# Three attention layers of 16 heads x 8: maxima by halves of 8 heads, one clamp per head, weights on three semaphores

## What is computed

```python
# L0 cross attention (512 keys, 96 wide); x is (8, 256, 128), 16 heads of 8
q = (layernorm(x) @ Wq + bq).reshape(B, Nq, H, D).transpose(0, 2, 1, 3)
k = (ctx @ Wk + bk).reshape(B, Nkv, H, D).transpose(0, 2, 1, 3)
v = (ctx @ Wv + bv).reshape(B, Nkv, H, D).transpose(0, 2, 1, 3)
attn = jnp.einsum('bhqd,bhkd->bhqk', q, k) * D ** -0.5
attn = jnp.clip(attn, -10000.0, 10000.0)
attn = jax.nn.softmax(attn, axis=-1)
x = x + jnp.einsum('bhqk,bhkd->bqhd', attn, v).reshape(B, Nq, Cq) @ Wo + bo
```

## Time and profile before

| | us |
|---|---|
| median of 3 runs | 2920.61 |
| lowest, highest | 2910.09, 2923.78 |
| the profiled execution | 2914.34 |
| its span, first to last instruction | 2912.6 |

### The profile page before, as it was taken

How to read it: one execution, slowest core, us unless ns; L and a number is a source line. 1 busy time by engine, 2 the same in 40 slices (tenths; PEclk the granted TensorE clock), 3 DMA queues, 4 the chain that set the end, 5 groups by cost and what they waited for, 6 DMA issues and landing times. The chain is left out here.

```text
span 2912.6 us, 40706 instructions
## 1 busy us (share of the span) xinstructions
PE 2224.6 (76%) x13779; PEld 1382.4 (47%) x13779; DVE 1690.1 (58%) x3810; ACT 1174.3 (40%) x2898; POOL 522.7 (18%) x703
## 2 busy tenths in 40 slices
PE   4668888789996897534799994936888886898982
PEld 2424343367774454423566663625555654344441
DVE  5568999633434562877456556562665554754524
ACT  3114444445552564211344441410555553354550
POOL 1122220000002410121111101011333322212100
PEclk9759999899997898866899997965999998698995
DMA  0043323110002310000000001011000001332200
GB/s 27 12 116 86 115 77 92 50 40 1 1 1 62 76 46 28 8 0 0 31 1 1 1 1 28 1 27 34 1 1 1 1 1 38 85 75 63 53 11 17
DMA packets 109272, 95.63 MB, mean 33 GB/s; under 512 B 61414, under 2 KB 96526, under 8 KB 105742
## 3 DMA queue, kind: packets, MB, share of 16 engines
q1 hardware_dynamic: 75790, 91.99, 12.2%
q10 hardware_dynamic: 33280, 1.05, 0.5%
HBM read 77.21 MB, written 14.81 MB: 32 GB/s over the span
## 5 line engine op out<-in xcount | busy, mean ns | idle before, releaser
L920 DVE TENSOR_REDUCE L_xattn_mx<-L_xattn_psS 128x1 f32<-128x512 f32 x512 | 326.9, 684 | 152.9 <-PE L_xattn_psS L1045 148.7
L1160 ACT ACTIVATE L_xattn_PT<-L_xattn_psT 128x512 f32<-128x512 f32 x512 | 284.7, 598 | 170.8 <-PE L_xattn_psT L1057 163.6
L1071 PE MATMUL L_xattn_psO<-L_xattn_PT,L_xattn_V 128*32 128x256 f32 x2048 | 264.1, 404 | 40.8 <-DVE L_xattn_PT L931 40.8
L588 ACT ACTIVATE L_attn_pr<-L_attn_psS,L_attn_negm 128x256 f32<-128x256 f32 (+1 forms) x512 | 222.4, 447 | 175.4 <-PE L_attn_psS L511 92.0
L1045 PE MATMUL L_xattn_psS<-L_xattn_KR,L_xattn_QR 72*128 72x512 bf16 x512 | 224.0, 441 | 56.3 <-DVE L_xattn_mx L920 30.0
L1057 PE MATMUL L_xattn_psT<-L_xattn_QR,L_xattn_KR 75*128 75x256 bf16 x1024 | 198.7, 283 | 3.0 <-ACT L_xattn_PT L1160 2.0
L1875 DVE TENSOR_TENSOR L_ffn_wt<-L_ffn_act,L_ffn_cw 128x512 f32<-128x512 f32 x128 | 88.5, 692 | 183.8 <-ACT L_ffn_act L1992 172.4
L1071 PEld LDWEIGHTS L_xattn_psO<-L_xattn_PT,L_xattn_V 128*32 128x32 f32 x2048 | 118.4, 115 | 154.6 <-issue 61.2
L931 DVE SCALAR_TENSOR_TENSOR L_xattn_PT<-L_xattn_PT,L_xattn_floor_w 128x512 f32<-128x512 f32 x256 | 178.4, 741 | 16.1 <-DMA L_xattn_floor_w<-L_xattn_staged_floor 11.6
L392 DVE TENSOR_REDUCE L_attn_mx<-L_attn_psS 128x2 f32<-128x512 f32 x256 | 164.4, 684 | 40.0 <-PE L_attn_psS L501 40.0
L415 DVE TENSOR_TENSOR L_attn_aoT<-L_attn_raw,L_attn_psOR 128x256 f32<-128x256 f32 x128 | 54.0, 422 | 222.7 <-ACT L_attn_raw L601 222.7
(11 more groups left out here) (537 smaller groups left out, 4342.8 us busy)
## 6 DMA issues: line engine op xcount, KB each, us to landing
L_xattn_KR<-L_xattn_k_parts SPq DMA_DIRECT2D x96, 192.0 KB
L_xattn_floor_w<-L_xattn_staged_floor SPq DMA_DIRECT2D x8, 2048.0 KB, 8.2
L_xattn_QR<-L_xattn_q_parts SPq DMA_DIRECT2D x32, 288.0 KB
L_xattn_k_parts<-L_xattn_ks SPq DMA_DIRECT2D x48, 128.0 KB, 2.6
L_xattn_ctxT<-in_ctx SPq DMA_DIRECT2D x24, 192.0 KB, 2.4
L_attn_QR<-L_attn_q_parts SPq DMA_DIRECT2D x16, 288.0 KB
L_attn_KR<-L_attn_k_parts SPq DMA_DIRECT2D x48, 96.0 KB
L_xattn_q_parts<-L_xattn_qs SPq DMA_DIRECT2D x48, 64.0 KB, 2.5
```

Of the source, the lines that this page charges most:

```text
L588: ins = nc.scalar.activation(pr[n % 3][:, r, t, 0:width], psS[(2 * n + r) % 3][:, t, 0:width], ACT.Exp, bias=negm[:, n % 4, t, r:r + 1], s ...
L920: nc.vector.reduce_max(mx[:, b % 2, u, hd:hd + 1], psS[n % 2][:], AX.X).then_inc(s_used, 1)
L1071: ins = nc.tensor.matmul(psO[r:r + HW, g % 2], V[b % NV][:, kt, n % H], PT[(n * NU + kt // 2) % NPT][:, kt % 2], start=(kt == 0), stop=(kt ...
L1160: nc.scalar.activation(PT[i % NPT][:], psT[i % NPS][:], ACT.Exp).then_inc(exp_ready, 1)
```

## The change

It is made of these parts:

- LEAD goes from H to HH = 8 heads plus the same margin: 14 instead of 22 (18 instead of 26 in L1); PREP from 42 to 38 (60 to 52).
- Job M and the rows are done twice a batch, each for 8 heads. The half i is at step 16b + 8i - 5 (16b + 8i - 9 in L1). negm, mp, floor and floor_w are half as high; the rows have a semaphore for each half.
- In from_ctx layers the order is K, T, Q instead of T, Q, K, with K at 16b - 38, T one step behind it and Q two; stage and spread take k first. Stage is at 16b - 33. Within a step M is sorted behind the other jobs.
- A PT tile holds a head's four key tiles, five of them instead of ten half as large, and one clamp covers 1024 columns.
- The weights have three semaphores: for q and k, for v, and for the output. PE waits for each ahead of its first use.
- POOL sets V[0] between norm(0) and norm(1), and the other V tiles behind DVE's splits of the first batch. It adds bo at Q instead of K.

```diff
...
-    NPS, NPT = 3, 10 if NU == 2 else 8
+    NPS, NPT = 3, 5 if NU == 2 else 8
...
-    LEAD, PREP, STAGE, DVE_SPLITS = (H + 6, 42, 3, 2) if from_ctx else (H + 10, 60, 6, 3)
+    LEAD, PREP, STAGE, DVE_SPLITS = (HH + 6, 38, 3, 2) if from_ctx else (HH + 10, 52, 6, 3)
...
         at = prep_step(b)
-        for i, kind in enumerate("TQK"):
+        for i, kind in enumerate("KTQ" if from_ctx else "TQK"):
             jobs[at + i * (b > 0)].append((kind, b, 0))
         jobs[max(H * b - LATE_V, FIRST) if from_ctx else at + 3 * (b > 0)].append(("V", b, 0))
-        jobs[H * b - LEAD + H + 1].append(("M", b, 0))
+        for i in range(2):
+            jobs[H * b + HH * i - LEAD + HH + 1].append(("M", b, i))
         for i in range(NO):
...
-        stage_at = at + 2 + STAGE if b else FIRST
+        stage_at = min(at + 2 + STAGE, prep_step(b + 1) + 1) if b else FIRST
         moves[stage_at].append(("stage", b, 0))
         moves[max(stage_at, H * (b - NB + 1) + 1)].append(("spread", b, 0))
-        moves[H * b - LEAD + H + 1].append(("rows", b, 0))
+        for i in range(2):
+            moves[H * b + HH * i - LEAD + HH + 1].append(("rows", b, i))
         if head_major:
...
-    jobs[FIRST].sort(key=lambda job: job[1])
+    for n in jobs:
+        jobs[n].sort(key=lambda job: (job[0] == "M", job[1] if n == FIRST else 0))
...
-        negm, mp = sb("negm", [H, S]), sb("mp", [H, PARTS, S], BF16)
-        PT = [sb(f"PT{i}", [P, 2, S]) for i in range(NPT)]
+        negm, mp = sb("negm", [HH, S]), sb("mp", [HH, PARTS, S], BF16)
+        PT = [sb(f"PT{i}", [P, NKT, S]) for i in range(NPT)]
...
-        floor, floor_w = (sb("floor", [H, S]), [sb(f"floor_w{i}", [P, H, S]) for i in range(2)]) if clamp else (None, None)
-        minus_clamp = sb("minus_clamp", [H, 1]) if clamp else None
-        f_dram = nc.dram_tensor(f"{pre}_staged_floor", (H, S), F32, kind="Internal").ap() if clamp else None
+        floor, floor_w = (sb("floor", [HH, S]), [sb(f"floor_w{i}", [P, HH, S]) for i in range(2)]) if clamp else (None, None)
+        minus_clamp = sb("minus_clamp", [HH, 1]) if clamp else None
+        f_dram = nc.dram_tensor(f"{pre}_staged_floor", (HH, S), F32, kind="Internal").ap() if clamp else None
...
-        NLOAD = 8 if bq is not None else 5
+        WQK, WV = (4, 2) if bq is not None else (2, 1)
...
+            loads = [(wk_s[:], m.dram[wk], qk_loaded), (wq_s[:], m.dram[wq], qk_loaded)]
...
+            loads += [(wv_s[:], m.dram[wv], v_loaded), (wo_s[:], m.dram[wo], o_loaded), (bo_s[:], rows(m.dram[bo]).to_broadcast((P, D)), o_loaded)]
+            for dst, src, done in loads:
+                sp.dma_start(dst, src).then_inc(done, 16)
...
+                if from_ctx:
+                    stage_k()
+                    stage_q()
+                else:
+                    stage_q()
+                    stage_k()
...
+                for hf in range(2):
+                    heads, done = slice(hf * HH, (hf + 1) * HH), regrouped[b % 2][hf]
+                    if from_ctx:
+                        spread_k(heads, done)
+                        spread_q(heads, done)
+                    else:
+                        spread_q(heads, done)
+                        spread_k(heads, done)
...
+            def max_rows(b, hf):
+
+                n = 2 * b + hf
                 wait(sp, st_ready, NU * H * (b - NB + 1))
-                sp.wait_ge(m_split, b + 1)
+                sp.wait_ge(m_split, n + 1)
                 for i in range(PARTS):
-                    sp.dma_start(QR[b % NB][PAIR + i:PAIR + i + 1], mp[:, i]).then_inc(m_rows, 16)
...
                     sp.dma_start(f_dram, floor[:]).then_inc(floor_staged, 16)
-                    sp.wait_ge(floor_staged, 16 * (b + 1))
...
+                    wait(sp, clamped, HH * (n - 1))
+                    sp.dma_start(floor_w[n % 2][:].rearrange("p h s -> p (h s)"),
+                                 rows(f_dram.rearrange("h s -> (h s)")).to_broadcast((P, HH * S))).then_inc(floor_spread, 16)
...
-            def split_max(b):
-
-                pool.wait_ge(negm_ready, b + 1)
+            def split_max(n):
+
+                pool.wait_ge(negm_ready, n + 1)
                 if clamp:
                     link(nc.gpsimd.tensor_scalar(negm[:], negm[:], clamp, None, ALU.min))
                     nc.gpsimd.sem_inc(clamp_set, 1)
+                    if n >= 1:
+                        pool.wait_ge(m_rows[(n - 1) % 2], 16 * PARTS * ((n - 1) // 2 + 1))
                     link(nc.gpsimd.tensor_copy(mp[:, 0], negm[:]))
-                    pool.wait_ge(floor_ready, b + 1)
...
             norm(0)
+            nc.gpsimd.memset(V[0][:], 1.0).then_inc(v_set, 1)
             norm(1)
-            for i in range(NV):
+            pool.wait_ge(k_split, SPLITS)
+            pool.wait_ge(q_split, SPLITS)
+            for i in range(1, NV):
                 nc.gpsimd.memset(V[i][:], 1.0).then_inc(v_set, 1)
...
                     if kind == "T" and b >= 2:
                         norm(b)
                     if kind == "Q" and b >= DVE_SPLITS:
                         split_q(nc.gpsimd, link, b)
                     if kind == "K" and b >= DVE_SPLITS:
                         split_k(nc.gpsimd, link, b)
-                    if kind == "K":
+                    if kind == "Q":
                         add_bo(b)
                     if kind == "M":
-                        split_max(b)
+                        split_max(2 * b + i)
...
-                b, hd = n // NU // H, n // NU % H
-                dve.wait_ge(exp_ready, n + 1)
-                if n % (NU * H) == 0:
-                    dve.wait_ge(floor_spread, 16 * (b + 1))
+                half = n // HH
+                dve.wait_ge(exp_ready, NU * (n + 1))
+                if n % HH == 0:
+                    dve.wait_ge(floor_spread, 16 * (half + 1))
                 at = PT[n % NPT][:]
-                nc.vector.scalar_tensor_tensor(at, at, 1.0, floor_w[b % 2][:, hd, None, :].to_broadcast((P, 2, S)), ALU.min, ALU.max).then_inc(clamped, 1)
-
-            def bound_max(b):
-
...
+            def bound_max(b, i):
+
+                await_job(dve, ("M", b, i))
+                wait(dve, m_split, 2 * b + i)
+                nc.vector.tensor_scalar(negm[:], psM[0:HH, 0:S], -1.0, -clamp, ALU.mult, ALU.max).then_inc(psM_read, 1)
+                await_read(dve, ("M", b, i))
...
-            pe.wait_ge(loaded, 16 * NLOAD)
-
...
-                    pe.wait_ge(s_used, NSU * (b + 1))
+                    pe.wait_ge(s_used, NSU * b + NSU // 2 * (i + 1))
...
+                if b == 0 and kind in "QK":
+                    pe.wait_ge(qk_loaded, 16 * WQK)
+                if b == 0 and kind == "V":
+                    pe.wait_ge(v_loaded, 16 * WV)
+                if b == 0 and kind == "O":
+                    pe.wait_ge(o_loaded, 16 * 2)
...
-                        ins = nc.tensor.transpose(psM[0:H, t * P:(t + 1) * P], mx[:, b % 2, t], m.ident[:])
+                        ins = nc.tensor.transpose(psM[0:HH, t * P:(t + 1) * P], mx[:, b % 2, t, i * HH:(i + 1) * HH], m.ident[:])
...
-                if hd == 0 and u == 0:
-                    pe.wait_ge(m_rows, 16 * PARTS * (b + 1))
+                if hd % HH == 0 and u == 0:
+                    pe.wait_ge(m_rows[hd // HH], 16 * PARTS * (b + 1))
...
+                        if n >= NPT:
+                            act.wait_ge(pv_done, (n - NPT) // 2 + 1)
+                        nc.scalar.activation(PT[n % NPT][:, 2 * u:2 * u + 2], psT[i % NPS][:], ACT.Exp).then_inc(exp_ready, 1)
...
```

More of the change, by code:

```diff
@@ L762, in spread, with spread_q @@
             def spread(b):
                 wait(sp, st_ready, NU * H * (b - NB + 1))
[L765 to L767 removed]
+                def spread_q(heads, done):
+                    sp.wait_ge(q_staged, 16 * PARTS * (b + 1))
                     src = q_dram[b % 2].rearrange("i d h c -> (i d) h c")[:, heads]
[L769 removed]
+                    sp.dma_start(QR[b % NB][0:PAIR, heads], src[:, None].to_broadcast((PARTS * DH, PARTS, HH, S))).then_inc(done, 16)
@@ L770, in spread, with spread_k @@
+                def spread_k(heads, done):
                     sp.wait_ge(k_staged, 16 * PARTS * (b + 1))
@@ L984, in _ @@
                 if clamp and 1 <= n <= NH:
-                    for u in range(NU):
-                        clamp_probs((n - 1) * NU + u)
+                    clamp_probs(n - 1)
                 if n >= 11 and (n - 11) % 8 == 0 and (n - 11) // 8 < NH // 8:
@@ L1066, in weigh @@
                     wait(pe, ot_ready, g - 1)
-                pe.wait_ge(clamped if clamp else exp_ready, (first + 2) * NU)
+                pe.wait_ge(clamped if clamp else exp_ready, (first + 2) * (1 if clamp else NU))
                 for kt in range(NKT):
```

101 lines of the change are left out of this document (45 added, 56 removed).

## The result

The changed kernel takes **2954.4 us** (median of 4 runs, 2950.7 to 2958.2) beside 2918.3 for the kernel before on the same chip: a ratio of 1.0127, 95% interval 1.0107 to 1.0147. So it is slower by 36 us by the medians (37 by the ratio), where 2980 had been forecast, some 60 more than before. The profiled execution took 2950.7 us, its span is 2949.0; against the profiled execution of before that is 36 us more.

What follows compares the result with a forecast made beforehand. DVE was taken to set the pace in L0's steady stage, PE in L3's. Terms sum to +61.5 us on the profiled 2914.3, so 2976; 6.3 for the runs' median gives 2982, forecast 2980 (2950 to 3010; 8 in 10: 2943 to 3018).

Steps and rivals of the forecast that it cites:

- T(2): Starts of L0 and L3: the turn of batch 2 stands behind split_k(2), +6.1 us in each.
- jobs that share a step: L3: V and K share a step and PE waits between them for DVE's four adds, +5 us (0 to 8).
- second chain: Maxima done twice a batch: +14 us in L0 (8 to 21), +9 in L3 and L1 (5 to 14).
- SP's queue: L3: a later stage lets the read-back of the heads' outputs land in time, -13 us (-17 to 0).
- start: Each layer's start: earlier weights for K and a quicker DVE cast save 3.5 us, -10.5 in all (-6 to -15).
- lead and floors: Eight heads' maxima leave each start, floors come earlier; with the starts' T(2) waits -9 us (-20 to +3).
- wide clamp: L0: one clamp of 1024 columns saves 0.06 us a head over 114 heads, -7 us (0 to -20).
- The wait at T: L0 and L3, b = 3 to 7: norm(b) behind split_k(b) on POOL makes PE wait 6.1 us, ten times, +61 (+51 to +73).
- The clock behind it: PE's granted clock falls after each of ten pauses, 1.2 us each, +12 us (0 to +30).
- Rival 1: The wait at T is hidden, 78 us of the sum are gone: 2904 us, faster than before; chance 8%.
- Rival 2: The wait grows by late floors or rows or a lower clock, 4 us more in ten batches: 3020 us; chance 11%.
- Rival 3: First scores hang on the same DMAs of q and k, the start gets no shorter: 2996 us; chance 5%.

Runs made afterwards that it cites:

- kernel 1: The changed kernel with norm(b) moved ahead of split_k(b) on POOL, at K's step, in the layers that read the context: 2879.5 us, 0.9881 of before.
- 11: kernel 1 with K, T and Q four steps earlier (PREP 42) and the stage kept at 16b - 33: 2851.2 us, 0.9787 of before.
- kernel 5: kernel 1 with the old lead back, 22 and 26 steps in place of 14 and 18: 2900.6 us.
- 6: kernel 5 with one chain of maxima per batch, of 16 heads, its floors spread at once: 2896.6 us.
- kernel 7: The kernel before with stage(b) four steps later in the two layers that read the context: 2892.8 us, 0.9917 of before.
- kernel 8: The kernel before with the weights on three semaphores and POOL's memsets placed as in the change: 2901.3 us, 0.9952 of before.
- kernel 3: The kernel before with one clamp of 1024 columns a head in place of two of 512, PT in five tiles: 2906.9 us, 0.9975 of before.
- 4: The changed kernel with a spare memset on POOL ahead of norm(b), b = 3 to 7, in the layers that read the context: 2972.2 us.
- kernel 2: The kernel before with only the order K, T, Q in the layers that read the context, add of bo at the last job: 3013.5 us, 1.0342.
- 12: Kernel 11 with one chain of maxima per batch and the old lead of 22 and 26 steps: 2863.8 us, 0.9839 of before.
- run 9: kernel 1 with K, T and Q, and the stage with them, two steps later (PREP 36) in the layers that read the context: 2864.3 us.

## Why the prediction was right, and where its terms were not

The forecast was slower by some 60 us through one mechanism. The sign and the mechanism hold; the size came out at 36, at the low end of the forecast's own range of 2950 to 3010. Term by term, in us:

| term of the sum | forecast | measured | from |
|---|---|---|---|
| norm behind split_k: ten waits, T(2) in two starts, the clock behind them | 61 + 12 + 12 = 85 | 75 | after less kernel 1 |
| jobs that share a step (V with K, T with M) | 5 | 28 | kernel 1 less 11, where others share |
| second chain | 23 | 4 | kernel 5 less 6 |
| SP's queue and the read-back | -13 | -25 | kernel 7 |
| start | -10.5 | -16 | kernel 8 |
| lead and floors, without T(2) | -21 | -21 | kernel 1 less 5, the lead alone |
| wide clamp | -7 | -10 | kernel 3 |
| sum | +61.5 | +35 | measured +36 |

Each measured term is a difference of medians and uncertain by 4 us (the clamp) to 10, and the second, third and sixth were taken beside others of the change. That the sum meets the result to 1 us is partly luck, and proves no single term.

- **The wait at T** was the right step. The forecast joined K's chain and the norm end to end, 8.4 us, and took 6.1 for PE's wait; it is 6.39 in L3 and 7.27 in L0. That 6.1 is so near in L3 is two errors that nearly cancel: from K to T it is 7.9 us and not 8.4, and PE stands at T after 1.5 us and not after 2.3. In L0 PE stands there after 2.0 us, and DVE's clamp stretches POOL's cast, which the forecast had only in its upper end of 7.3. Five of each and two in the starts are there, as said. Rival 1, that it is hidden, fails by runs 1 and 4. Its sum was wrong as it stood: the 78 us took in the 5 of V and K, which don't hang on T, and left out the 12 of T(2) in the starts; by the forecast's own terms 85 us would have gone, to 2897.
- **The clock behind it** was one of the mis-sized terms. In L3 the busy time of the same matmuls falls by 4.1 us over four batches when the pauses go, so 1.0 a batch against the 1.2 taken; in L0 by 1.2, so 0.3. That is 5.5 us less over ten pauses. It depends on the company: between kernel 2 and the kernel before it is 2.6 a batch in L0 and 1.4 in L3. Another 1.4 us of each pause came back as other waits (-14), the pauses themselves were longer than 6.1 (+7), the starts' two cost 10.5 instead of 12.2, and L1 was 3 us shorter in kernel 1 with the same code, which is scatter: 85 - 5.5 - 14 + 7 - 2 + 3 is some 74.
- **V and K in one step** was the term most in error: 5 us, for L3 alone. The rows of kernel 1 show PE waiting 4.3 us for V at K and 5.4 us for ACT's copy of hT at M, over four batches of L0, and nearly the same in L3, with the clock down to 0.93 and 0.95 in their wake. The prediction saw the first and put the second only inside L0's wait at T. Of the 28 us some 22 lie in the ten steady batches by these stretches and 5 in the two starts.
- **The second chain**: nearly right in size where little else waits (1.65, 0.3 and 1.0 us a batch between kernels 11 and 12) and wrong for the changed kernel, where it is felt as 4 us in all. DVE's maxima wait equally long for scores with one chain or with two there. Why the second is not felt has not been shown; I would look at T's step, where the one chain waits as well.
- **SP's queue**: the mechanism held and the size was half. I had costed the waits of 3.33 us and left out the clock that the earlier trace rows show behind one, though I charged it for the waits that come.
- **Start**: 16 instead of 10.5, just beyond the end of its bounds at 15. In L0 it is the wait for the weights that was sized too small: 3.6 us where half of 3.9 had been taken. That leaves 1.0 of the 4.6 us for the cast and all else.
- **Lead and floors**: the equal numbers, 21 and 21, are chance. The forecast's are 16.3 for the lead and 4.7 for the earlier floors. Kernel 5 keeps the floors by halves, so its 21 are the lead alone; no run has the floors by themselves.
- **Rival 2** (floors or rows late) did not come: the clamps wait 6.3 us for floors, 11.6 before. **Rival 3** neither: 22.0 us from L0's first instruction to its first scores instead of 26.7.

Five of the six errors made the forecast too high, by some 50 us together, and one, the largest, made it 23 too low. So the nearness of 2980 to 2954 is in part luck. The sign is not: it hangs on the wait behind split_k, 75 us where 85 had been taken, and without that term the measured sum is 40 us faster than before. The clock behind a wait was counted on one side of the sum only.

## What to carry to other kernels

When jobs are reordered on one engine, follow the same reorder through every other engine's list: the loss lay in POOL's list, in a job that had been early by accident, and moving one line there turned 1.3% slower into 1.2% faster. Jobs that pass through one PSUM bank make PE wait when they share a step, and by how much depends on which jobs these are. Ask what each step holds on the other engines before moving a job there: run 9 freed K and T of V and M, and put the norm behind the split of the maxima. And in a stage that PE bounds, price a pause with the clock behind it, on both sides of the sum.
